# Expert blocks of two independent 128-row units, the second unit's weights copied into a ring for each pass

## The chip, the cores and the metric

The kernel runs on one core of one Trainium2 chip. The metric is the device time of one execution in microseconds (us), as the median of repeated runs. The trace is one execution taken by the hardware profiler; its engines are PE (matrix multiply; PEld is its weight load), DVE (vector), ACT (scalar activations), POOL (GpSimd) and SP, whose work here is to issue DMAs.

## The reference, cut to what matters

An input of 32 x 16 x 32 tokens of 128 channels (16,384 tokens) goes through a masked agent attention, a linear attention, and a mixture of eight experts, each with a residual. The change touches the experts alone. Of each token the router takes the two best of eight experts, and the reference adds both experts' outputs with softmax weights:

```python
logits = x @ router_w + router_b
top_w, sel = jax.lax.top_k(logits, TOP_K)            # TOP_K = 2
tok_w = zeros((T, E)).at[arange(T)[:, None], sel].add(softmax(top_w))
def body(acc, params):                               # for each of the E = 8 experts
    gu = x @ Wgu + bgu                               # 128 -> 2 x 256
    gate, up = jnp.split(gu, 2, axis=-1)
    act = (up + 1.0) * quick_gelu(gate)
    out = act @ Wd + bd                              # 256 -> 128
    return (acc + out * w_e[:, None], None)
```

## The kernel before

The kernel has three stages, one after the other, with a barrier of all engines between them: `agent_attention`, `token_mixer`, `experts`. Eight experts give 28 pairs. In `token_mixer` each token's row (128 channels and five words: two norm factors, two shares, its own number) is scattered by POOL (L810) into a DRAM tensor `rows`, in which every pair has a region of its own. Behind the last token of each region 256 rows of "nobody" are written (`tails`, L714 to L721, 14 regions from SP's queue and 14 from ACT's), so that the last block of a region is full. DVE then works out a small table (L1206 to L1238): `first_i`, where each block's rows start, and `word_i`, in which the experts of five blocks are packed as digits.

`experts` runs over 92 blocks of 256 rows, all of one pair. A block takes two passes, one for each expert of its pair, so there are 184 passes, k = 0 to 183. The engines are driven by `in_turns`: position p of the schedule holds on PE the transposes of a block's rows (`xT`, lag 1, every second position), the inner matmuls of pass p-2 (`inner`, L1366 to L1368) and the outer matmuls of pass p-4 (`outer`, L1378 to L1384). Eight positions are a turn; two turns are one iteration of the hardware loop. At the start of a turn PE reads the turn's word of experts (`look_up`, L1339). Weights are kept as a high and a low fp16 part, so a product is three matmuls. An inner pass is 12 matmuls of 256 columns, an outer pass 14 of 128 columns: for each of the two 128-row halves one for the bias and six for the hidden part. The weights' address in SBUF comes from a register, so one stationary tile serves a whole block.

DVE's `result` (L1465, lag 5) weighs a pass's output and adds it to the row. After the second pass of a block POOL scatters the block's two halves to the output (`send`, L1315 and L1318), which counts a semaphore `r_out` of the block's slot. There are eight slots. SP's `load` (L1293 to L1296) looks up a block's first row, waits for the slot's `r_out` of eight blocks earlier, and issues one DMA of 256 rows into the slot; ACT normalises them (L1400) and PE transposes them (L1351). SP's queue holds nothing else in this stage.

Of the kernel before, what the change touches and what calls it, by code (L numbers as in the profile page):

```python
# [15 lines left out]
ALU = mybir.AluOpType  # L16
# [18 lines left out]
BLOCK = 256  # L35
REGION = B * TOK + BLOCK
BLOCKS = 92
TURN = 8
TURNS = 2 * BLOCKS // TURN
SLOTS = 8  # L40
BEHIND = 4
WORDS = TURNS + 1
RSTD, SHIFT, WLO, WHI, WHO = C, C + 1, C + 2, C + 3, C + 4
ROW = C + 5
LN_STEPS, ROUTE_STEPS, EXP_STEP, PLACE_STEPS, COLUMN_STEP = 7, 14, 9, 10, 26
# [5 lines left out]
assert BLOCKS >= (B * TOK - G) // BLOCK + G and 2 * BLOCKS % TURN == 0 and TURNS % 2 == 1  # L51
# [6 lines left out]
def _constants():  # L58
# [23 lines left out]
    put(1, "next_pair", np.tile(packed[1:] - packed[:-1], (P, 5)))  # L82
    looked = (TURN * r[:, None] - BEHIND) // 2 + np.arange(5)[None, :]
    put(1, "block_no", np.concatenate([looked, r[:, None]], 1) * 1.0)
    put(1, "block_row", r[:, None] * float(BLOCK))
# [558 lines left out]

def token_mixer(nc, cst, resid, ones16, ident, mixer, ffn, rows_dram, gate_up, gate_up_bias, down, down_bias):
# [4 lines left out]
    w1_hl, w2_hl, b2_hl = ffn["w1_hl"], ffn["w2_hl"], ffn["b2_hl"]  # L650
    wall, wrow, st1 = mixer["wall"], mixer["wrow"], mixer["st1"]
    with ExitStack() as ctx:
# [41 lines left out]
        over = sb("m_over", [P, 6, G])  # L694
        found = sb("m_found", [P, 6, G])
        look = sb("m_look", [P, 6])
        cnt, cnti, nb, delta = sb("m_cnt", [P, G]), sb("m_cnti", [P, G], I32), sb("m_nb", [P, G]), sb("m_delta", [P, G])
        cum = sb("m_cum", [P, 2, G])
        word_i = sb("m_word_i", [1, WORDS], I32)
# [14 lines left out]
        b2_row = b2_hl[:].rearrange("p e c -> p (e c)")  # L714

        def tails(eng, first):

            eng.wait_ge(s.table, 2)
            for g in range(first, G, 2):
                row = eng.value_load(ffn["tail_i"][0:1, g:g + 1], min_val=g * REGION, max_val=(g + 1) * REGION - BLOCK)  # L720
                eng.dma_start(rows_dram[bass.ds(row, BLOCK)].rearrange("(n p) w -> p n w", p=P), ffn["nobody"][:]).then_inc(s.nobody_in, 16)  # L721
# [4 lines left out]
        def _(sp):  # L726
# [16 lines left out]
            sp.dma_start(rows_dram[G * REGION:G * REGION + BLOCK].rearrange("(n p) w -> p n w", p=P), ffn["nobody"][:]).then_inc(s.nobody_in, 16)  # L743
# [4 lines left out]
        def _(pool):  # L748
            g = nc.gpsimd
            g.memset(half[:], -0.5).then_inc(s.set_g, 1)  # L750
            g.memset(b2_hl[:], 0.0).then_inc(s.b_zero, 1)
# [26 lines left out]
            def biases_low(k, ring):  # L778

                if not isinstance(k, int) or k != 2:  # L780
                    return
                pool.wait_ge(s.bh_done, 1)
                g.tensor_tensor(b2_f[:], b2_f[:], b2_row[0:1, :], ALU.subtract).then_inc(s.bl_done, 1)
# [35 lines left out]
        def _(act):  # L819
# [14 lines left out]
            def biases(k, ring):  # L834
# [6 lines left out]
                if k == 1:  # L841
                    act.wait_ge(s.bf_done, 1)
                    act.wait_ge(s.b_zero, 1)
                    a.activation(b2_row[0:1, :], b2_f[:], ACT.Copy).then_inc(s.bh_done, 1)
                if k == 3:
                    act.wait_ge(s.bl_done, 1)
                    a.activation(b2_row[32:33, :], b2_f[:], ACT.Copy).then_inc(s.bh_done, 1)
# [77 lines left out]
        def _(pe):  # L925
# [108 lines left out]
            for n, column in enumerate((0, 1, 5)):  # L1034
                last = t.transpose(banks_o[0:1, 0, n * P:(n + 1) * P], look[:, column:column + 1], ident)
# [3 lines left out]
        def _(dve):  # L1039
# [30 lines left out]
            v.memset(ffn["nobody"][:].bitcast(I32)[:, :, WHO:WHO + 1], int(NO_SLOT)).then_inc(s.nobody_set, 1)  # L1070
# [137 lines left out]
            step(v.tensor_scalar(cnti[:], cnt[:], float(BLOCK - 1), None, ALU.add))  # L1208
            step(v.tensor_scalar(cnti[:], cnti[:], BLOCK.bit_length() - 1, None, ALU.arith_shift_right))
            step(v.tensor_copy(nb[:], cnti[:]))  # L1210
            step(v.tensor_scalar(delta[:], nb[:], -float(BLOCK), float(REGION), ALU.mult, ALU.add), False)
# [6 lines left out]
            all_pairs = [P, 6, G]  # L1218
            number = const(cst, "block_no").rearrange("p (n o) -> p n o", o=1).to_broadcast(all_pairs)
            step(v.tensor_tensor(over[:], number, now.rearrange("p (o g) -> p o g", o=1).to_broadcast(all_pairs), ALU.is_ge))  # L1220
            step(v.tensor_tensor(found[:, 0:5, :], over[:, 0:5, :], const(cst, "next_pair").rearrange("p (n g) -> p n g", n=5), ALU.mult), False)
            step(v.tensor_tensor(found[:, 5, :], over[:, 5, :], delta[:], ALU.mult))
            step(v.tensor_reduce(look[:], found[:], AX.X, ALU.add))

            step(v.tensor_scalar(look[:, 0:5], look[:, 0:5], 1.0, None, ALU.add), False)
            step(v.tensor_tensor(look[:, 5:6], look[:, 5:6], const(cst, "block_row"), ALU.add))
            step(v.tensor_scalar(look[:, 5:6], look[:, 5:6], float(G * REGION), None, ALU.min), False)
            step(v.scalar_tensor_tensor(look[:, 0:1], look[:, 1:2], 64.0, look[:, 0:1], ALU.mult, ALU.add))
            step(v.scalar_tensor_tensor(look[:, 0:1], look[:, 2:3], 4096.0, look[:, 0:1], ALU.mult, ALU.add), False)
            step(v.scalar_tensor_tensor(look[:, 1:2], look[:, 4:5], 64.0, look[:, 3:4], ALU.mult, ALU.add))  # L1230
            dve.wait_ge(s.col_psum, 1)
            row = banks_o[0:1, 0]
            word = ffn["word_i"]
            step(v.tensor_copy(ffn["first_i"][:], row[:, 2 * P:2 * P + BLOCKS]), False)
            step(v.tensor_copy(word[:], row[:, 0:WORDS]), False)
            step(v.tensor_copy(word_i[:], row[:, P:P + WORDS]))
# [5 lines left out]
def in_turns(eng, *stages, look=None):  # L1242
# [11 lines left out]
    with eng.Fori(0, TURNS // 2) as two:  # L1254
# [267 lines left out]
```

## Time and profile before

| | |
|---|---|
| median of 3 runs | 1207.85 us (1205.22 to 1208.79) |
| profiled execution | 1216.59 us, its span 1214.8 us |
| `agent_attention`, `token_mixer`, `experts`, us from the span's start | 0 to 371, 371 to 763, 763 to 1214.8 |
| PE busy over the span | 1034.6 us, 85% |
| DVE busy | 891.0 us, 73% |
| ACT busy | 714.4 us, 59% |
| POOL busy | 583.1 us, 48% |
| DMA | 64.18 MB, mean 53 GB/s |

The span is 1.8 us less than the profiled execution, which is 8.7 us above the median. A busy share is an average over three stages of different kinds; what the last stage is bound by is read in the last stage.

### The profile page before, as it was taken

What the parts mean: (1) busy time and instruction counts of PE and PEld (TensorE: products, weight loads), DVE (VectorE), ACT (ScalarE), POOL (GpSimd) and SP (SyncE); (2) the same over time, 40 slices, a digit from 0 to 9 for tenths busy, and PEclk for the clock granted to TensorE, in tenths of its full rate; (3) what the DMA queues carried; (4) which work ended last, traced back from release to release, by engine and by line L of the source; (5) the groups of instructions that cost most, each with busy time, mean ns of one, the idle gap of its engine ahead of it and who ended that gap; (6) DMA issues with size and microseconds to landing.
All of it is one profiled execution on the core that took longest, in us unless ns stands there. A gap on an engine that the chain in (4) does not pass through costs nothing. (4 is left out here: it accounts for less than half of the span.)

```text
span 1214.8 us, 39840 instructions
## 1 busy us (share of the span) xinstructions
PE 1034.6 (85%) x12967; PEld 857.2 (71%) x12968; DVE 891.0 (73%) x2181; ACT 714.4 (59%) x1446; POOL 583.1 (48%) x630
## 2 busy tenths in 40 slices
PE   5799999999986887888887840699999999999995
PEld 4477877787763456666666740588888898888984
DVE  5687777777773347877877762488888888888985
ACT  1277665666643257676676620567676767676763
POOL 0425746374676215555655552144444444444443
PEclk9899999999997778999999965799999999999998
DMA  8011101011103001111211219221112111221110
GB/s 308 26 38 28 38 21 35 21 37 29 29 3 105 18 18 41 59 58 59 68 51 60 65 56 142 55 57 50 52 55 56 51 52 48 56 56 52 35 23 1
DMA packets 72324, 64.18 MB, mean 53 GB/s; under 512 B 9812, under 2 KB 58227, under 8 KB 72237
## 3 DMA queue, kind: packets, MB, share of 16 engines
q1 hardware_dynamic: 57132, 43.46, 13.3%
q0 software_dynamic: 10016, 17.16, 4.6%
q10 hardware_dynamic: 5090, 2.32, 1.5%
q8 instruction: 64, 1.05, 0.4%
q14 instruction: 22, 0.18, 0.1%
HBM read 33.44 MB, written 24.72 MB: 48 GB/s over the span
## 5 line engine op out<-in xcount | busy, mean ns | idle before, releaser
L1318 POOL DMA_INDIRECT out<-e_y,e_xg x184 | 183.7, 998 | 77.8 <-issue 77.6
L1366 PE MATMUL e_ps<-e_xt,w_hl 128*128 128x256 f16 x736 | 202.2, 275 | 14.2 <-issue 12.8
L1367 PE MATMUL e_ps<-e_xt,w_hl 128*128 128x256 f16 x736 | 201.8, 274 | 0.0
L1368 PE MATMUL e_ps<-e_xt,w_hl 128*128 128x256 f16 x736 | 201.7, 274 | 0.0
L810 POOL DMA_INDIRECT rows<-m_rows,m_place x128 | 127.5, 996 | 44.4 <-issue 44.4
L251 POOL TENSOR_SCALAR vm<-v,early 128x512 f32<-128x512 f32 x96 | 148.5, 1562 | 0.0
L1383 PE MATMUL e_ps<-w_hl,e_hid_hl 128*128 x736 | 145.6, 220 | 0.0
L1384 PE MATMUL e_ps<-w_hl,e_hid_hl 128*128 x736 | 144.9, 219 | 0.0
L1382 PE MATMUL e_ps<-w_hl,e_hid_hl 128*128 x736 | 144.1, 220 | 0.0
L1443 DVE SCALAR_TENSOR_TENSOR e_hid_hl<-e_hid,e_hid_hl 128x512 f16<-128x512 f32 x184 | 127.4, 692 | 20.0 <-ACT e_hid_hl L1416 19.7
L1437 DVE SCALAR_TENSOR_TENSOR e_hid<-e_ps,e_act 128x512 f32<-128x512 f32 x184 | 125.9, 684 | 15.2 <-ACT e_act L1422 10.9
L1416 ACT ACTIVATE e_hid_hl<-e_hid 128x512 f16<-128x512 f32 x184 | 115.2, 626 | 16.6 <-DVE e_hid L1437 7.0
L1422 ACT ACTIVATE e_act<-e_ps 128x512 f32<-128x512 f32 x184 | 107.8, 586 | 9.9 <-PE e_ps L1368 9.8
L1400 ACT ACTIVATE e_xn<-e_xg 128x128 f32<-128x128 f32 x184 | 80.2, 489 | 42.1 <-DMA e_xg<-rows 42.1
L249 POOL TENSOR_TENSOR vm<-v,early 128x512 f32<-128x512 f32 x32 | 33.2, 1039 | 135.5 <-PE ps L447 132.3
L1315 POOL TENSOR_TENSOR e_held<-e_one 1x1 f32<-1x1 f32 x92 | 18.3, 199 | 162.9 <-DVE e_y L1465 162.9
L1409 ACT ACTIVATE e_xt<-e_ps 128x256 f16<-128x256 f32 x92 | 35.2, 383 | 102.5 <-PE e_ps L1351 102.5
L1366 PEld LDWEIGHTS e_ps<-e_xt,w_hl 128*128 x736 | 72.2, 98 | 28.6 <-issue 18.4
L286 ACT ACTIVATE km<-ps,bk_pair,early 128x512 f32<-128x512 f32 x128 | 89.1, 789 | 0.0
L1378 PE MATMUL e_ps<-b_hl,e_ones 128*128 x368 | 80.6, 219 | 0.7 <-DVE e_hid_hl L1443 0.7
L1368 PEld LDWEIGHTS e_ps<-e_xt,w_hl 128*128 x736 | 72.4, 98 | 8.8
L1367 PEld LDWEIGHTS e_ps<-e_xt,w_hl 128*128 x736 | 72.4, 98 | 6.8
(249 smaller groups left out, 2603.6 us busy)
## 6 DMA issues: line engine op xcount, KB each, us to landing
e_xg<-rows SPq DMA_DIRECT2D x92, 133.0 KB
resid<-in_x SPq DMA_DIRECT2D x8, 1024.0 KB, 13.9
xb<-in_x SPq DMA_DIRECT2D x32, 256.0 KB, 2.7
m_rows<-resid SPq DMA_DIRECT2D x32, 256.0 KB, 2.7
out<-e_y,e_xg POOLq DMA_INDIRECT x184, 2.3
m_w_f<-in_L_ffn_gate_up_proj SPq DMA_DIRECT2D x1, 2048.0 KB, 8.2
rows<-m_rows,m_place POOLq DMA_INDIRECT x128, 2.4
rows<-nobody SPq DMA_DIRECT2D x15, 133.0 KB, 10.0
```

What stands on the lines that cost most here:

```text
L251: ins = g.tensor_scalar(vm[:, u, :, n, :], full, pair_of[:, n:n + 1], None, ALU.mult)
L810: g.indirect_dma_start(rows_dram, bass.IndirectOffsetOnAxis(ap=place[:, slot, j:j + 1], axis=0), rows[:, slot, j, :], None).then_inc(s.row ...
L1318: nc.gpsimd.indirect_dma_start(out_rows, bass.IndirectOffsetOnAxis(ap=who, axis=0), y[:, slot, i, :], None, bounds_check=B * TOK - 1, oob_ ...
L1366: t.matmul(o, hi, x2[0], start=True, stop=False)
L1367: t.matmul(o, hi, x2[1], start=False, stop=False)
L1368: last = t.matmul(o, lo, x2[0], start=False, stop=True)
L1382: t.matmul(o, hi, whi, start=False, stop=False)
L1383: t.matmul(o, hi, wlo, start=False, stop=False)
L1384: last = t.matmul(o, lo, whi, start=False, stop=q == 1)
L1416: a.activation(hid_hl[:, i, 0].rearrange("p q n -> p (q n)"), hid[:, i], ACT.Copy, scale=1.0 / (WS * QG)).then_inc(s.hh_done, 1)
L1437: v.scalar_tensor_tensor(hid[:, i], ps[:, 4 + i], WS, act_g[:, i], ALU.add, ALU.mult).then_inc(s.hid_done, 1)
L1443: v.scalar_tensor_tensor(hid_hl[:, i, 1].rearrange("p q n -> p (q n)"), hid[:, i], 1.0 / (WS * QG), hid_hl[:, i, 0].rearrange("p q n -> p ...
```

## The change

A unit is now 128 rows of one pair. A block is still 256 rows and two passes, but it is any two units, whose pairs need not agree. There are 78 blocks (156 units, 156 passes) in place of 92 blocks (184 passes). The tail of nobody rows is 128 rows for each region.

The two halves of a block may need different experts in one pass. The first half takes its weights as before, by a register. For the second half SP copies one expert's packed weights (1664 fp16 numbers on each of 128 partitions, 416 KB in all) from `weights` to one of eight places of a ring `e_fed`, once for each pass; PE waits for that copy before the pass's inner matmuls. Of a block, SP loads the two halves with a DMA each, each with its own look-up, which now stands behind the wait for `r_out`. The copies of block b stand in SP's queue behind the load of block b+4 (`LEAD = 4`), and each waits for the outer matmuls of eight passes earlier.

The inner matmuls become 24 of 128 columns for each pass (12 of 256 before); the outer ones stay 14 of 128. The table gets two starts for each block and a second word for each turn: twelve searched columns in place of six, six small transposes in place of three, three more steps on DVE.

```diff
+UNIT = 128
-BLOCK = 256
-REGION = B * TOK + BLOCK
-BLOCKS = 92
+BLOCK = 2 * UNIT
+REGION = B * TOK + UNIT
+BLOCKS = 78
+LEAD = 4
...
         def tails(eng, first):
...
-                eng.dma_start(rows_dram[bass.ds(row, BLOCK)].rearrange("(n p) w -> p n w", p=P), ffn["nobody"][:]).then_inc(s.nobody_in, 16)
+                eng.dma_start(rows_dram[bass.ds(row, UNIT)], ffn["nobody"][:]).then_inc(s.nobody_in, 16)
...
             def load(n, slot, rounds):
 
-                row = sp.value_load(ffn["first_i"][0:1, n:n + 1] if isinstance(n, int) else ffn["first_i"][0:1, bass.ds(n, 1)],
-                                    min_val=0, max_val=G * REGION)
                 need(sp, r_out[slot], 32 * rounds)
-                sp.dma_start(xg[:, slot], rows_dram[bass.ds(row, BLOCK)].rearrange("(n p) w -> p n w", p=P)).then_inc(x_in[slot], 16)
+                for half in range(2):
+                    row = sp.value_load(ffn["first_i"][0:1, half, at(n)], min_val=0, max_val=G * REGION)
+                    sp.dma_start(xg[:, slot, half], rows_dram[bass.ds(row, UNIT)]).then_inc(x_in[slot], 16)
+
+            def second_words(turn):
+
+                return sp.value_load(ffn["word_i"][0:1, 1, at(turn)], min_val=0, max_val=64 ** 5 - 1)
+
+            def second_weights(k, ring, word, digit):
+
+                e = (word // 8 ** (digit + 1 - 2 * (digit % 2))) % 8
+                need(sp, s.y_psum, k - TURN + 1)
+                sp.dma_start(fed[:, ring:ring + 1], ffn["weights"][:, bass.ds(e, 1)]).then_inc(fed_in[ring], 16)
+
+            def eight(m, first, last, loads):
+
+                word = None
+                for i in range(first, last):
+                    if i < loads:
+                        load(SLOTS * m + i, i, m)
+                    if i < LEAD and isinstance(m, int) and m == 0:
+                        continue
+                    turn = -1 if i < 3 else 0 if i < 7 else 1
+                    if word is None or i in (3, 7):
+                        word = second_words(2 * m + turn)
+                    for u in range(2):
+                        far = 2 * (i - LEAD) + u
+                        second_weights(2 * SLOTS * m + far, far % TURN, word, far - TURN * turn + BEHIND)
...
-                x2 = [xt[:, slot % 2, l, :] for l in range(2)]
+                pe.wait_ge(fed_in[j], 16 * (2 * rounds + slot // 4) + 16)
...
+                        for half in range(2):
+                            x2 = [xt[:, slot % 2, l, half * P:(half + 1) * P] for l in range(2)]
+                            o = ps[:, bank + i, q * BLOCK + half * P:q * BLOCK + (half + 1) * P]
+                            if half:
+                                hi, lo = (w1_fed[:, j, l, at:at + P] for l in range(2))
```

On SP's queue, inside the loop over blocks, this is what stood for one block before (`first_i` is the table of starts, `e_xg` the slots' rows, `e_r1_out` the count of slot 1's scatters):

```order
L1293 ISA
L1293 TENSOR_LOAD first_i
L1293 ISA x2
L1296 ISA [waits e_r1_out]
L1296 DMA e_xg<-rows 128x2x133
```

Now the same place reads as follows (`e_fed` is the ring, `e_y_psum` counts PE's outer passes; left out is the second half's look-up, which repeats the first's).

```order
L1314 ISA [waits e_r1_out]
L1314 TENSOR_LOAD first_i
L1314 ISA x2
L1315 ISA
L1315 DMA e_xg<-rows 128x133
...
L113 REGISTER_ALU
L1325 ISA [waits e_y_psum]
L1325 DMA e_fed<-weights 128x1664
L113 REGISTER_ALU
L1325 ISA [waits e_y_psum]
L1325 DMA e_fed<-weights 128x1664
```

The look-up has moved behind the wait for the slot, there are two loads, and two copies of weights stand behind them; in three blocks of eight a look-up of the word of experts (`word_i`) stands between loads and copies.

On PE this is the start of an inner pass before (`e_act_done` says that a bank of PSUM is free):

```order
L110 REGISTER_ALU [waits e_xl_done,e_xh_done]
L1366 ISA [waits e_act_done]
L1366 MATMUL e_ps<-e_xt,w_hl 128x256
L1367 MATMUL e_ps<-e_xt,w_hl 128x256
L1368 ISA
L1368 MATMUL e_ps<-e_xt,w_hl 128x256
```

and now (`weights` holds the eight experts, `e_fed4_in` counts the landings of the ring's fifth place):

```order
L113 REGISTER_ALU [waits e_fed4_in,e_xl_done,e_xh_done]
L1413 ISA [waits e_act_done]
L1413 MATMUL e_ps<-e_xt,weights 128x128
L1414 MATMUL e_ps<-e_xt,weights 128x128
L1415 ISA
L1415 MATMUL e_ps<-e_xt,weights 128x128
L1413 MATMUL e_ps<-e_xt,e_fed 128x128
L1414 MATMUL e_ps<-e_xt,e_fed 128x128
L1415 MATMUL e_ps<-e_xt,e_fed 128x128
```

Each matmul has become two of half the width, and the wait for the copy stands ahead of the pass's first matmul, with all later work of PE behind it.

## Rows read from the trace of the kernel before

**Rows 1.** Stretches: us, busy us by engine (instructions), PE clock granted, DMA share, GB/s.
```profile
0.00:30.00 30.00, 15.72 (x93) 11.93 (x94) 15.90 (x41) 3.48 (x5) 1.32 (x6) 1.00 0.86 312
488.00:709.00 221.00, 180.36 (x1252) 145.99 (x1250) 175.10 (x654) 144.64 (x347) 125.69 (x159) 0.98 0.19 59
780.00:1200.00 420.00, 407.15 (x4861) 371.47 (x4859) 370.18 (x810) 294.68 (x626) 197.22 (x270) 1.00 0.18 48
```

**Rows 2.** Timeline of PE, one pass (start us, us); the page's inner weight loads (ns).
```profile
906.19 0.27 PE L1366 MATMUL e_ps<-e_xt,w_hl 128*128 128x256 f16 x1
...
907.50 0.22 PE L1378 MATMUL e_ps<-b_hl,e_ones 128*128 x1
...
908.28 0.39 PE L1351 MATMUL e_ps<-early,e_xn 128*128 128x128 f32 x2
908.51 0.27 PE L1366 MATMUL e_ps<-e_xt,w_hl 128*128 128x256 f16 x1
...
L1366 PEld LDWEIGHTS e_ps<-e_xt,w_hl 128*128 x736 | 72.2, 98 | 28.6 <-issue 18.4
```

**Rows 3.** Timelines of PE: the first inner matmul of block 0 and of block 91.
```profile
769.29 0.39 PE L1366 MATMUL e_ps<-e_xt,w_hl 128*128 128x256 f16 x1 [1.33 <-DVE e_xt L1451]
...
1194.96 0.28 PE L1366 MATMUL e_ps<-e_xt,w_hl 128*128 128x256 f16 x1 [0.41 <-issue]
```

**Rows 4.** Timelines of PE, DVE, POOL, SP: block 27's end, the load that waits for it.
```profile
901.78 0.27 PE L1366 MATMUL e_ps<-e_xt,w_hl 128*128 128x256 f16 x1
...
906.58 0.34 DVE L1465 SCALAR_TENSOR_TENSOR e_y<-e_ps,e_xg,e_y 128x128 f32<-128x128 f32 x1
...
907.99 1.00 POOL L1318 DMA_INDIRECT out<-e_y,e_xg  x1 [0.54 <-issue]
909.29 0.98 POOL L1318 DMA_INDIRECT out<-e_y,e_xg  x1 [0.30 <-issue]
...
911.72 0.37 SPq L1296 DMA_DIRECT2D e_xg<-rows  x1
...
915.50 0.28 PE L1366 MATMUL e_ps<-e_xt,w_hl 128*128 128x256 f16 x1 [0.33 <-issue]
```

**Rows 5.** Lines of SP: ns min/median/max, first and last start us; then two starts.
```profile
L1293 SPq TENSOR_LOAD <-first_i x92: 263/268/281, 763.3 to 1168.4; - x92
L1296 SPq DMA_DIRECT2D e_xg<-rows x92: 371/373/1047, 764.1 to 1172.6; - x92
...
764.07 0.41 SPq L1296 DMA_DIRECT2D e_xg<-rows  x1
772.73 0.37 SPq L1296 DMA_DIRECT2D e_xg<-rows  x1
```

**Rows 6.** DMA landings: of `e_xg` (min/median/max us); on the page, count, KB, median us.
```profile
DMA to landing us min/median/max: 2.1/2.3/3.7
...
xb<-in_x SPq DMA_DIRECT2D x32, 256.0 KB, 2.7
m_rows<-resid SPq DMA_DIRECT2D x32, 256.0 KB, 2.7
```

**Rows 7.** Nobody rows: SP's lines, landings, SP's wait; the DMA of 728 to 766.
```profile
L720 SPq TENSOR_LOAD <-tail_i x14: 278/372/565, 729.0 to 745.9; - x14
L721 SPq DMA_DIRECT2D rows<-nobody x14: 372/372/413, 729.9 to 746.6; - x14
DMA to landing us min/median/max: 3.1/10.3/16.3
SPq L652 <- DMA rows<-nobody: 15.9, 1, 15.9
DMA packets 8210, 4.65 MB, mean 122 GB/s; under 512 B 624, under 2 KB 8048, under 8 KB 8208
rows<-m_rows,m_place POOLq DMA_INDIRECT x9, 9.6
```

**Rows 8.** Timeline of POOL: its last scatter of rows in `token_mixer`.
```profile
741.14 0.96 POOL L810 DMA_INDIRECT rows<-m_rows,m_place  x1 [0.30 <-issue]
```

## What the change will do, predicted before any run of it

> **What bounds the kernel now.** I read the stretches first, then PE's timeline in the last stage, then the one other thing that the change leans on there, SP's queue. From 780 to 1200 us PE is busy 407 of 420 us at the full granted clock, DVE 370, ACT 295, and the DMA engines 18% of the time at 48 GB/s [rows 1]. So the last stage is PE's, with DVE close behind and much room in the DMA engines. One pass on PE: the twelve inner matmuls run from 906.19 to 907.50, 1.31 us or 109 ns each; the fourteen outer ones from 907.50 to 908.28, 0.78 us or 56 ns each; a block's two transposes take 0.23 us [rows 2]. Two passes and the transposes are 4.41 us. Block 0 starts its inner matmuls at 769.29 and block 91 at 1194.96 [rows 3]: 425.7 us over 91 intervals, 4.68 us a block. The 0.27 us over 4.41 is lost where a turn begins and PE reads its word.
>
> The second thing to see is how late a slot comes free. In one steady block, 27, DVE begins the last result at 906.58, 4.80 us after PE started the next block's inner matmuls at 901.78; POOL issues the two scatters at 907.99 and 909.29, and SP's load that waits for them starts at 911.72, 5.14 us after the result [rows 4]. That wait costs nothing today: the rows loaded there are used almost four blocks later. PE starts block 31, four later, at 915.50, 8.9 us after that result [rows 4].
>
> **The change, part by part.** Fewer blocks. If PE stayed the bound, 77 intervals would take the place of 91. A pass has 24 inner matmuls of 128 columns at the 56 ns of the outer ones, 1.34 us in place of 1.31; a block grows by 0.06 to 4.74, and 77 of them are 365 us, 61 us less than now.
>
> A rule speaks against that pitch. The Trainium skill, TensorE: Matmul & The Clock Gate, section Back-to-back issue gap, says that a stream of weight load and matmul pairs of 128 columns sustains about 81 ns each. The fourteen pairs of an outer pass run at 56 ns here, so the trace does not agree, and by the rule it is a rival below.
>
> The copies and their place in SP's queue. This is the step on which I expect the gain to be lost. Copies of block b stand behind the load of block b+4, which waits for the scatters of block b-4. So PE may not start block b until a chain has run from the last result of block b-4. Its links:
> - to the point where SP's first load of the block would start: 5.14 us [rows 4].
> - SP's own work. In the start of the stage, where loads wait for nothing, eight loads start between 764.07 and 772.73; seven intervals are 8.66 us, and one of the DMAs took 1.05 in place of 0.37, so an undisturbed load with its look-up is (8.66 - 0.67) / 7 = 1.14 us [rows 5]. The look-up is some 0.62 of it (1.14 less the DMA's 0.37 and about 0.15 of register steps and gaps), and it moves behind the wait. Then comes the second half's load, which I take at 1.10 (half the pieces), 0.6 until the first copy starts, and in three blocks of eight a look-up of the word, 0.62 x 3/8 = 0.23. Together 2.55.
> - the copy's landing. A load of 133 KB lands after 2.3 us, copies of 256 KB from DRAM or within SBUF after 2.7 [rows 6]. At 312 GB/s with the engines 86% busy [rows 1] the DMA moves 363 GB/s, so 416 KB (426,000 bytes) take 1.17 us, 0.45 more than 256 KB: 3.15 by that, 2.3 as the lower end. No row shows a 416 KB copy; I take 2.9, nearer to the copy within SBUF, whose rows are in four times as many pieces.
> - 0.2 us until PE's first matmul, and 0.2 because copies and scatters now share the engines (estimates; the second is one 0.2 us piece of a scatter's data).
>
> The sum is L = 5.14 + 2.55 + 2.9 + 0.4 = 11.0 us. The last result of block b-4 begins A = 4.8 us after the start of block b-3 [rows 4], 4.9 with the longer inner passes and PE's restart behind a wait. So block b starts at least A + L = 15.9 us after block b-3: three blocks take 15.9, one takes 5.30. PE alone needs 4.74, which would allow L up to 3 x 4.74 - 4.9 = 9.3. PE therefore waits about 0.55 us in each block, and 77 x 5.30 = 408.1 replace 425.7: **-17.6 us** in place of -61. Queued behind the waiting matmul are all of PE's later work and through it DVE, ACT and POOL; as the chain runs through them, it does not catch up.
> The second copy of a block starts 0.6 us after the first and is needed a pass (2.2 us) later, so it hides. The DMA engines carry two copies (2.35 us) and today's 18% in 5.3 us, some 60%: not the bound.
>
> The start of the stage. SP's first look-up starts at 763.3, its first load at 764.07 [rows 5], PE's first inner matmul at 769.29 [rows 3], 6.0 later. Now the first copy stands behind five blocks' loads: 0.73 + nine intervals of 1.10 + 0.37 for the last DMA, then the word 0.65 and 0.2 to the copy, 11.85; with 2.9 to land and 0.2 for PE 14.95. **+9.0 us**. Nothing hides it, as no other work is there yet. Later copies of the first four blocks come at 1.7 us a pass or less and keep ahead of PE.
>
> The nobody rows. SP's last of fourteen DMAs starts at 746.6, but SP waits 15.9 us for their landings, up to 762.9 [rows 7]. In 728 to 766 us 4.65 MB moved, of which 28 x 0.136 = 3.8 MB are nobody rows; the queue is late because of bytes. Half of them leave 2.75 MB. If the data took 30.5 us (from about 730 to 2 us before the wait ends), they take 18 now and end near 748, 2 us later landed: 750. SP's own issue ends at 746.6 less 14 x 0.04, plus 3.1 for the shortest landing, 749; POOL's last scatter starts at 741.14 and lands in 9.6 at today's load [rows 7, 8], 750.7, and no later with less load. The barrier opens about 750.5 in place of 763: **-12.5 us**, between -14 and -9.
>
> The table. Three more steps, wider searches and three more transposes are 1 to 2 us on DVE and PE that end near 740, under the nobody rows that end at 750; uncovered they would cost 2 us. The strided weights cost nothing that I can name, and the end of the kernel is as before.
>
> **Sum.** -17.6 + 9.0 - 12.5 = -21.1 us. The profiled execution of 1216.6 becomes 1195.5; it stands 8.7 above the median, so the median becomes **1187 us**.
>
> **Bounds.** Lower: landing 2.3, no sharing, 0.1 for PE: L 10.1, A 4.8, 4.97 a block, 383 us; with the rest -46, or 1162. Upper: landing 3.7 (the longest of a load), look-ups at the 0.565 us seen under a loaded queue in place of 0.27 [rows 7], 2.4 of them, and scatters 0.5 later: L 12.8, A 5.0, 5.93 a block, 457 us, +31 + 9 - 9 = +31, or 1239.
>
> **Rivals.**
> The copies are hidden. Then 365 us, -61 + 9 - 12.5 = -64, 1143 us. It needs L under 9.3; 5.14 and SP's 2.55 alone are 7.7, and no DMA in the rows lands in 1.4.
> Slower, by the same chain. The whole gain is gone when a block takes 425.7 + 3.5 over 77, 5.57 us, which is from L = 11.8 on. Loaded look-ups and landings of 3.4 us are enough: L 12.4, 5.77 a block, 444 us, +18.6 + 9 - 12.5 = +15, 1223 us. For it speaks that look-ups doubled under load; against it that the engines are 40% free.
> Weight loads that show. A load takes 98 ns [rows 2] and hides behind 109 ns of an inner matmul now. If in a stream of 24 pairs it did not hide, inner passes would be 24 x 98 = 2.35 us and a block 6.5, over the chain's 5.3: 500 us, +75 + 9 - 12.5 = +71, 1279 us. The outer passes hide the same loads behind 56 ns. By the page's 81 ns a block would be 6.4 us, much the same.
> PE's clock falls. Waiting 0.55 us in each block, PE is busy some 85%; between 488 and 709 us it was busy 82% at a mean granted clock of 0.98 [rows 1]. If a tenth of the stage ran at 1.2 GHz, where a block's 4.5 us of matmuls doubles, that tenth would take 8 x 9.3 us for 8 x 5.3: +32, 1219 us.
> That the change does less work than it says can't be: the number of blocks is fixed in the loops.
>
> **Chances.** Chain as summed 0.66 (1164 to 1208 us), hidden 0.06, slower by the chain 0.17, weight loads 0.05, clock 0.06. The range leaves out the hidden case, the weight loads and the far end of the slow ones: 1164 to 1219. About 0.3%, 3.6 us, is what a measurement of this kernel can tell from no change. Inside 1204.2 to 1211.5 lies a part of the chain's case and of the slower one, 0.09; faster 0.69, slower 0.22.
>
> **What would show it.** Right: PE's inner matmuls of a block's first pass wait about 0.55 us for a DMA of `e_fed`, every block alike from block 4 on; blocks 5.3 us apart; a result 15.9 - 4.9 = 11 us ahead of the inner matmul four blocks later; the barrier at 750; the first inner matmul 15 us behind it. Wrong: no waits of PE on `e_fed` and blocks 4.74 apart (the chain is shorter than its rows); matmuls 80 ns apart; waits on every pass, and the DMA share near one (bytes); a clock under one.

## The result, and the profile after

The changed kernel takes 1222.7 us (median of 4 runs, 1217.1 to 1223.9) where the kernel before took 1207.1 beside it (4 runs, 1205.2 to 1208.8): a ratio of 1.0121, 95% interval 1.0085 to 1.0156. A second set of runs on another chip gave 1.0105, 1.0082 to 1.0128. The change is slower by about 1.1%, outside the predicted range and on the other side of zero. The profiled execution took 1222.6 us with a span of 1220.7; before, the span was 1214.8.

The last stage, by stretch. The columns are those of [rows 1].

```profile
780.00:1200.00 420.00, 352.07 (x5664) 334.79 (x5662) 306.06 (x654) 244.93 (x510) 158.69 (x217) 0.97 0.53 193
```

PE was busy 407 of these 420 us before [rows 1], and is busy 352 now; no other engine is near its limit, and the DMA engines are 53% busy. So nothing is full, and something is late. What is late is in the list of waits of the same stretch (engine, line, what ended the wait: us in total, times, longest).

```profile
POOL e_held L1357 <- DVE e_y L1516: 200.9, 73, 6.0
ACT e_xt L1460 <- PE e_ps L1393: 93.8, 70, 2.7
PEld e_ps L1413 <- issue: 77.9, 59, 3.2
ACT e_act L1473 <- PE e_ps L1415: 64.8, 49, 3.9
POOL out L1360 <- issue: 61.3, 144, 2.0
PE e_ps L1413 <- DMA e_fed<-weights: 55.8, 37, 3.1
```

The last line is the one to read: PE waits for a copy of the weights 37 times, 1.5 us each, in the 73 blocks of the stretch. POOL (through DVE), ACT and the weight loads wait for PE in turn.

PE's first inner matmul of block 0, and then that of block 77, from PE's timeline (start us, us; in brackets the idle time before it):

```profile
761.62 0.29 PE L1413 MATMUL e_ps<-e_xt,weights 128*128 128x128 f16 x1 [9.96 <-DMA e_fed<-weights]
...
1203.35 0.22 PE L1413 MATMUL e_ps<-e_xt,weights 128*128 128x128 f16 x1
```

That is 441.7 us over 77 intervals, 5.74 us a block, against 425.7 us before [rows 3]. The prediction had 408.1 and 5.30.

One turn of the chain, from the timelines of PE, DVE, POOL, SP and PE again. Block 33 starts, block 32 gives its last result, its two scatters go, SP loads block 40, copies for block 36, and PE starts block 36:

```profile
953.62 0.23 PE L1413 MATMUL e_ps<-e_xt,weights 128*128 128x128 f16 x1 [1.56 <-DMA e_fed<-weights]
...
958.46 0.60 DVE L1516 SCALAR_TENSOR_TENSOR e_y<-e_ps,e_xg,e_y 128x128 f32<-128x128 f32 x2
...
959.88 1.00 POOL L1360 DMA_INDIRECT out<-e_y,e_xg  x1 [0.55 <-issue]
961.19 0.98 POOL L1360 DMA_INDIRECT out<-e_y,e_xg  x1 [0.30 <-issue]
...
965.07 1.55 SPq L1315 DMA_DIRECT2D e_xg<-rows  x2
967.62 1.31 SPq L1325 DMA_DIRECT2D e_fed<-weights  x2
...
970.85 0.23 PE L1413 MATMUL e_ps<-e_xt,weights 128*128 128x128 f16 x1 [0.19 <-issue]
```

From block 33's start to block 36's it is 17.23 us for three blocks, 5.74 each, which is the mean pace. Its parts are A = 958.46 - 953.62 = 4.84 and L = 970.85 - 958.46 = 12.39. The prediction named this ring and every link of it; it had L = 11.0. In the profile's records the copy for block 36 has landed at 970.53, and PE's matmuls of the blocks before end at 970.66 and leave 0.19 us of idle time: in this turn the copy and PE's own work come out almost together. Of the 61 blocks from 8 to 69 whose landing can be told, PE starts 42 within 0.6 us of the copy's landing, 0.41 us behind it on average; the others it starts later for reasons of its own, as where it reads its word.

Two more places answer to the rest of the sum. The nobody rows: SP's line, the landings, and SP's wait at the barrier, as in [rows 7].

```profile
L731 SPq DMA_DIRECT2D rows<-nobody x14: 332/332/381, 727.2 to 742.1; - x14
DMA to landing us min/median/max: 2.0/3.7/4.2
...
SPq L662 <- DMA rows<-nobody: 3.5, 1, 3.5
```

The wait fell from 15.9 us to 3.5 and the median landing from 10.3 to 3.7. And SP's look-ups of rows (ns min/median/max, first and last start) with the copies' DMAs and their landings:

```profile
L1314 SPq TENSOR_LOAD <-first_i x156: 264/290/894, 746.3 to 1179.7; - x156
...
L1325 SPq DMA_DIRECT2D e_fed<-weights x156: 485/496/1316, 758.5 to 1193.5; - x156
DMA to landing us min/median/max: 2.7/2.7/3.7
```

The first look-up is at 746.3, 17.0 us before the 763.3 of [rows 5]; PE's first inner matmul comes 15.3 us after it, where it was 6.0.

### The profile page after: what moved, and what is told of

Same layout as the page of the kernel before. It is cut to its first block and busy times, and to the rows that moved or that the text cites. A ratio compares the mean times of both kernels' runs of the same rounds, so it can differ in the third digit from the quotient of the medians.

```text
span 1220.7 us, 41928 instructions
## 1 busy us (share of the span) xinstructions
PE 995.1 (82%) x14086; PEld 837.9 (69%) x14087; DVE 841.5 (69%) x2058; ACT 673.9 (55%) x1348; POOL 552.6 (45%) x588
## 5 line engine op out<-in xcount | busy, mean ns | idle before, releaser
L1413 PE MATMUL e_ps<-e_xt,weights 128*128 128x128 f16 x624 | 139.6, 224 | 79.1 <-DMA e_fed<-weights 65.8
L1360 POOL DMA_INDIRECT out<-e_y,e_xg x156 | 155.7, 998 | 65.7 <-issue 65.7
L1488 DVE SCALAR_TENSOR_TENSOR e_hid<-e_ps,e_act 128x512 f32<-128x512 f32 x156 | 107.2, 687 | 86.7 <-PE e_ps L1415 66.4
L1415 PE MATMUL e_ps<-e_xt,weights 128*128 128x128 f16 x624 | 139.6, 224 | 0.0
L1415 PE MATMUL e_ps<-e_xt,e_fed 128*128 128x128 f16 x624 | 139.1, 223 | 0.0
L1414 PE MATMUL e_ps<-e_xt,e_fed 128*128 128x128 f16 x624 | 139.1, 223 | 0.0
L1413 PE MATMUL e_ps<-e_xt,e_fed 128*128 128x128 f16 x624 | 139.0, 223 | 0.0
L1414 PE MATMUL e_ps<-e_xt,weights 128*128 128x128 f16 x624 | 138.9, 223 | 0.0
L1413 PEld LDWEIGHTS e_ps<-e_xt,weights 128*128 x624 | 62.0, 99 | 93.0 <-issue 89.6
L1494 DVE SCALAR_TENSOR_TENSOR e_hid_hl<-e_hid,e_hid_hl 128x512 f16<-128x512 f32 x156 | 108.1, 693 | 16.7 <-ACT e_hid_hl L1467 15.8
L1467 ACT ACTIVATE e_hid_hl<-e_hid 128x512 f16<-128x512 f32 x156 | 97.7, 626 | 14.1 <-DVE e_hid L1488 7.1
L965 PE MATMUL m_ps<-wall,m_xt 128*128 128x256 f32 x256 | 67.6, 411 | 5.4 <-DVE m_kf L1132 5.3
L965 PEld LDWEIGHTS m_ps<-wall,m_xt 128*128 128x128 f32 x256 | 49.7, 204 | 24.2 <-issue 17.9
L1434 PE MATMUL e_ps<-weights,e_hid_hl 128*128 x312 | 64.6, 225 | 0.0
```

The lines of the kernel that those rows point to most:

```text
L965: last = t.matmul(banks_kv[:, j // 2, j % 2 * 2 * C:(j % 2 + 1) * 2 * C], xt[:, u, j * P:(j + 1) * P], wall[:, C:3 * C], start=True, stop= ...
L1360: nc.gpsimd.indirect_dma_start(out_rows, bass.IndirectOffsetOnAxis(ap=who, axis=0), y[:, slot, i, :], None, bounds_check=B * TOK - 1, oob_ ...
L1413: t.matmul(o, hi, x2[0], start=True, stop=False)
L1414: t.matmul(o, hi, x2[1], start=False, stop=False)
L1415: last = t.matmul(o, lo, x2[0], start=False, stop=True)
L1467: a.activation(hid_hl[:, i, 0].rearrange("p q n -> p (q n)"), hid[:, i], ACT.Copy, scale=1.0 / (WS * QG)).then_inc(s.hh_done, 1)
```

## The experiments

Each kernel was run beside the kernel before on the same chip. That kernel's median was 1207 us on the first chip and 1213 to 1216 on the others, so I compare kernels by us a block (first inner matmul of block 0 to that of block 77, over 77), which moves little from chip to chip: the changed kernel unaltered, on another chip, has 5.745.

> The changed kernel unaltered, on the chip of the run beside it: ratio to the kernel before 1.012 and 5.74 us a block if the first result holds from chip to chip.

Measured: 1225.95 us, ratio 1.0105 (1.0082 to 1.0128), 5.745 a block. The result holds.

**The place in SP's queue.** My theory was that the pace is the ring's length over the number of blocks in it. The first edit puts one block more into the ring:

```
                 for i in range(first, last):
-                    if i < loads:
-                        load(SLOTS * m + i, i, m)
                     if i < LEAD and isinstance(m, int) and m == 0:
+                        load(SLOTS * m + i, i, m)
                         continue
...
                         second_weights(...)
+                    if i < loads:
+                        load(SLOTS * m + i, i, m)
```

> The two copies of block b stand ahead of the load of block b+4 in SyncE's queue instead of behind it, so that they wait on the scatters of block b-5 and no longer on those of b-4. Theory (the ring of result, scatter, load, copy, inner matmul sets the pace: (4.9 + 12.4) / 3 = 5.77 us a block, measured 5.74): with one block more in the ring it would be 17.3 / 4 = 4.3, below what TensorE needs by itself, about 4.75; so 77 x (5.74 - 4.75) = 76 us go and the time is about 1147, with next to no wait of TensorE for a copy. Rival one (the 32 KB a partition that the copies move for each ring turn slow everything, whatever order): the same bytes in the same time, so above 1200. Rival two (the narrower matmuls of 128 columns set the pace): the same, about 1222.

Measured: 1160.5 us, ratio 0.953 (0.949 to 0.957), 4.92 us a block. The same copies of the same size, in another place of the queue, give back 63 us of the stage (77 x 0.82). Waits of PE on the copies, 780 to 1110 us:

```profile
PE e_ps L1414 <- DMA e_fed<-weights: 6.3, 6, 1.2
```

It is not the 4.75 that I expected; the last experiments take that up. The opposite edit is `LEAD = 5`, with the second turn of eight blocks written out:

```
-LEAD = 4
+LEAD = 5
...
             eight(0, 0, SLOTS, SLOTS)
-            with sp.Fori(1, BLOCKS // SLOTS) as m:
+            eight(1, 0, SLOTS, SLOTS)
+            with sp.Fori(2, BLOCKS // SLOTS) as m:
```

> The copies of block b stand behind the load of block b+5, which waits for the scatters of b-3: one block less in the ring (the second turn of eight blocks is written out, so that its waits are constants). Theory: 17.4 us of ring over two blocks in place of three, less up to 0.5 us a ring for copies and scatters that now meet less often: 8.4 to 8.7 us a block, 77 x (8.4 to 8.7 - 5.74) = 205 to 228 us more, 1428 to 1450. If the order in the queue were not the cause, the same as the changed kernel, or less, for fewer copies in the same time.

Measured: 1449.9 us in one run, 8.61 a block. From 780 to 1420 us PE's waits and the stretch (columns of [rows 1]):

```profile
PE e_ps L1414 <- DMA e_fed<-weights: 244.1, 35, 8.7
...
780.00:1420.00 640.00, 395.86 (x5645) 388.39 (x5642) 301.14 (x652) 241.65 (x508) 159.19 (x218) 0.79 0.35 127
```

Every second block waits some 7 us. Over blocks 8 to 69 the mean A is 5.79 and L 12.2, so the ring gives 18.0 / 2 = 9.0, and the measured mean there is 9.04. A is longer than in the changed kernel because PE comes back from such a wait at half clock: the mean granted clock is 0.79 here, and the matmuls of the block at 900.97 us stand 107 ns apart until 902.36. With two blocks in the ring 8.6, with three 5.74, with four 4.92 (where the ring alone would allow 4.3 and so no longer binds): the place in the queue sets the pace.

**The length of the ring.** Two edits shorten it and leave the order alone. The first looks both row numbers up ahead of the wait:

```
+                found = [sp.value_load(ffn["first_i"][0:1, half, at(n)], ...) for half in range(2)]
                 need(sp, r_out[slot], 32 * rounds)
                 for half in range(2):
-                    row = sp.value_load(ffn["first_i"][0:1, half, at(n)], ...)
-                    sp.dma_start(xg[:, slot, half], rows_dram[bass.ds(row, UNIT)]).then_inc(x_in[slot], 16)
+                    sp.dma_start(xg[:, slot, half], rows_dram[bass.ds(found[half], UNIT)]).then_inc(x_in[slot], 16)
```

> SyncE looks both row numbers up before it waits for the scatters, as the kernel before did; the copies stay behind the load. Theory: from the wake to the first load's issue 0.87 us falls to about 0.3, and from the first issue to the second 1.21 falls to about 0.5, so the ring loses about 1.2 us: (4.9 + 11.2) / 3 = 5.37 a block, 77 x 0.37 = 29 us less, about 1194. Rival one (bytes of the copies): no change, 1215 to 1225. Rival two (narrow matmuls): no change.

Measured: 1199.8 us, ratio 0.987 (0.985 to 0.989), 5.39 a block. L is 11.30 (mean over blocks 8 to 69), 1.07 less; a third of that is 0.36 and the pace fell by 0.35. Two look-ups moved ahead of a wait are worth 27 us of the stage, and turn the change from 1% slower into 1.3% faster than before.

The second leaves the order and the wait and takes the bytes away (in this kernel and the next two both units take the first unit's weights, lines that the cuts leave out):

```
-                sp.dma_start(fed[:, ring:ring + 1], ffn["weights"][:, bass.ds(e, 1)])...
+                sp.dma_start(fed[:, ring:ring + 1, 0:WB], ffn["weights"][:, bass.ds(e, 1), 0:WB])...
```

> Each copy moves only the 256 bytes a partition of the bias instead of 3,328, in the same place of SyncE's queue, and TensorE waits for it as before; both units take the first unit's weights, which is the part left out. It tells what the size of the copies costs from what their place in the queue costs. Theory: the ring stays, and loses only what the traffic adds to it, about 0.65 us on the scatters' landing and about 0.6 on the copy's own: (4.9 + 11.1) / 3 = 5.35 us a block, about 1192. If the traffic were the main cost, the pace would fall to TensorE's own, 4.7, and the time to about 1145; if it cost nothing, 5.74 and 1222.

Measured: 1180.8 us in one run, 5.18 a block, better than the 5.35 expected. The links of the ring, means over blocks 8 to 69 from the timelines, beside what the prediction had:

| link, us | predicted | changed kernel | small copies |
|---|---|---|---|
| last result to first load's DMA | 5.14 + 0.62 = 5.76 | 6.74 | 6.11 |
| first load to second | 1.10 | 1.23 | 1.21 |
| second load to first copy | 0.60 + 0.23 = 0.83 | 0.89 | 0.89 |
| copy's issue to PE's first matmul | 2.9 + 0.2 = 3.1 | 3.50 | 2.48 |
| allowed for sharing | 0.2 | in the links | in the links |
| L | 11.0 | 12.37 | 10.69 |
| A | 4.9 | 5.04 | 4.89 |
| (A + L) / 3 | 5.30 | 5.80 | 5.19 |

So the size of the copies is worth 1.68 us of L: 1.0 in the copy itself, 0.64 between result and load, 0.03 between the loads. The rest of the ring is order, and stays with copies of 32 KB. SP's look-ups of rows (780 to 1200 us) in the changed kernel, then with the small copies, and the small copies' landings:

```profile
L1314 SPq TENSOR_LOAD <-first_i x138: 264/301/894, 781.5 to 1179.7; - x138
...
L1314 SPq TENSOR_LOAD <-first_i x139: 263/277/422, 780.8 to 1139.1; - x139
DMA to landing us min/median/max: 1.7/1.8/3.4
```

**The traffic without the wait, and the matmuls alone.** In the next kernel PE takes the wait for the copy in `outer`, two passes later:

```
             def inner(k, n, j, slot, rounds):
-                pe.wait_ge(fed_in[j], 16 * (2 * rounds + slot // 4) + 16)
...
             def outer(k, n, j, slot, rounds):
                 need(pe, s.hl_done, k + 1)
+                pe.wait_ge(fed_in[j], 16 * (2 * rounds + slot // 4) + 16)
```

> Every copy is issued in the changed kernel's place and waited for, but by TensorE only ahead of the second product of the pass, some 5 us later than there, and both units take the first unit's weights. So the whole traffic stays and the ring gets slack. Theory: ring (4.9 + 12.4 - 5) / 3 = 4.1, under TensorE's own pace, so 4.9 us a block as where the copies stand ahead of the load, and first inner matmul sooner by 8 us: about 1150. If the traffic itself set the pace: above 5.3 a block, above 1185.

Measured: 1156.4 us in one run, 4.96 a block, with the full traffic (225 GB/s from 780 to 1110 us). The last kernel of this group drops the copies too:

```
-                need(sp, s.y_psum, k - TURN + 1)
-                sp.dma_start(fed[:, ring:ring + 1], ffn["weights"][:, bass.ds(e, 1)]).then_inc(fed_in[ring], 16)
+                return
```

> Leaves out the copies and the wait for them, and both units of a block take the first unit's weights (so the second unit's rows meet another pair's weights); the loads and the narrow matmuls stay. Theory: TensorE's own pace shows, about 4.75 us a block, and the start waits for no copy (first inner matmul about 7 us after SyncE's first look-up instead of 15.3): 1222 - 76 - 8 = about 1138. Rival two (narrow matmuls set the pace): 5.7 a block stays, about 1214.

Measured: 1137.8 us in one run, 4.71 a block, first inner matmul 6.7 us after the first look-up. From 780 to 1110 us PE is as busy as the kernel before is in that stretch (319.78 us):

```profile
780.00:1110.00 330.00, 320.90 (x5469) 312.73 (x5467) 289.20 (x633) 231.35 (x492) 153.66 (x210) 1.00 0.20 53
```

The matmuls of 128 columns cost what the prediction said (4.74). Of the 1.03 us a block between 4.71 and 5.74, 0.77 go when only the wait moves, and 0.26 stay with the copies, that is with their bytes or with SP's work of issuing them. They do not slow the matmuls as such: over blocks 8 to 69 four blocks of eight take 4.47 to 4.49 us with these copies as without any, and what is left lies in the blocks in which PE reads its word and the ones right behind.

**A version that beats both.** Copies of block b behind the load of block b+1 or b+2 wait for scatters of blocks long done, and go out early in the stage:

```
-LEAD = 4
+LEAD = 1
...
-                    turn = -1 if i < 3 else 0 if i < 7 else 1
-                    if word is None or i in (3, 7):
+                    turn = -1 if i < LEAD - 1 else 0 if i < LEAD + 3 else 1
+                    if word is None or i in (LEAD - 1, LEAD + 3):
```

> The copies of block b stand behind the load of block b+1, not b+4: they wait only for the ring slot of b-4 (its second product), and in the steady state for no scatter younger than block b-7's. The first copies go out after two loads instead of five. Theory: TensorE's own pace and its dearer look-ups, 4.8 to 4.9 us a block (as with the copies ahead of the load, 4.90), and a first inner matmul some 6 us sooner, 9 us behind SyncE's first look-up: 1160 - 6 - 4 = about 1150, a ratio of 0.946 to the kernel before. If something other than the place in the queue holds the copies, 1160 or more.

Measured: 1147.6 us (1146.0 to 1150.6), ratio 0.9454 to the kernel before, interval 0.9433 to 0.9475; 4.81 a block, first inner matmul 8.3 us behind the first look-up, and no wait of PE on a copy from 780 to 1120 us. One constant, with the look-up places that follow from it, turns a loss of 1.1% into a gain of 5.5%.

> The same with the copies of block b behind the load of b+2, which waits for the scatters of b-6. Theory: the pace of the kernel above within 0.1 us a block, the first inner matmul 2 us later than there: about 1152. It tells whether the slack that the order gives is used up at one block (as where the copies stand just ahead of the load of b+4) or more.

Measured: 1146.2 us in one run, 4.84 a block, first inner matmul 10.5 us behind the first look-up: the same kernel in time.

**What holds the pace then.** Where the copies stood ahead of the load, 4.92 was left instead of 4.71. Two things stood out there. SP no longer waits: from 780 to 1110 us its list of waits is one line, where the changed kernel has 68.5 us on the scatters. And PE's look-ups of its word are slow. SP's waits of the changed kernel, then of the kernel with the copies ahead of the load; PE's look-ups (780 to 1200 us, ns min/median/max) without copies, and with the copies ahead of the load:

```profile
SPq L1314 <- DMA out<-e_y,e_xg: 68.5, 40, 3.7
...
SPq L1325 <- PE e_ps L1436: 0.2, 1, 0.2
...
L1380 PEldq TENSOR_LOAD <-word_i x18: 297/300/367, 788.4 to 1108.4; - x18
...
L1382 PEldq TENSOR_LOAD <-word_i x18: 302/754/946, 796.9 to 1131.1; - x18
```

To take work from SP I packed a block's two row numbers into one word (the last two lines are shortened):

```
+            both = ffn["first_i"]
+            step(v.tensor_copy(both[:], firsts[:, 0:2, 0:BLOCKS]))
+            step(v.tensor_scalar(both[:, 0], both[:, 0], 7, None, ALU.logical_shift_right))
+            step(v.tensor_scalar(both[:, 1], both[:, 1], 5, None, ALU.logical_shift_left))
+            step(v.tensor_tensor(both[:, 0], both[:, 0], both[:, 1], ALU.bitwise_or))
...
+                two = sp.value_load(ffn["first_i"][0:1, 0, at(n)], ...)
+                for half, row in enumerate((two % 4096 * UNIT, two // 4096 * UNIT)):
```

> The same packing with the copies just ahead of the load of block b+4, where a block took 4.90 to 4.92 us. Two causes of the 0.2 over TensorE's own 4.70 are open: SyncE's own instructions, or TensorE's look-ups of the word, 0.72 us each in place of 0.31 while copies move (0.1 a block). If SyncE: 4.70 to 4.80 a block, about 1150. If only the look-ups: 4.90 and 1160 as before.

Measured, with the copies ahead of the load of b+4: 1151.1 us (1147.6 to 1155.3), ratio 0.947 (0.944 to 0.950), 4.82 a block, as the theory on SP had it. The pace is from one trace of each kernel, and the two intervals of the ratio touch. But PE's look-ups became fast in the same run (0.34 us on average, 0.72 without the packing), probably because copies that go out earlier no longer meet them. The look-ups' 0.38 us in every fourth block are 0.1 a block, as much as was gained. What was taken out of the stage is SP's second look-up alone, so SP's own instructions stand behind the gain; how much of the 0.1 was PE's look-up and how much a late copy stays open.

> As the run with the copies behind the load of block b+2, and the two row numbers of a block packed into one word (three more small VectorE steps in the table), so that SyncE looks up once a block. In that run, and where the copies stood ahead of the load, SyncE was without a wait almost throughout: its own instructions, about 4.8 us a block, kept pace with TensorE's. Theory: SyncE falls to about 4.1 us a block and TensorE alone sets the pace, 4.70 to 4.78 (4.835 before), with idle time again in SyncE's queue; start 0.6 us sooner: about 1141, ratio to the kernel before 0.940. If SyncE was not a bound: 4.83 and 1146 or more.

Measured: 1148.7 us (1146.4 to 1149.9, 5 runs), ratio 0.9462 (0.9439 to 0.9484), 4.80 a block. This expectation was wrong. SP has idle time again,

```profile
SPq L1329 <- PE e_ps L1439: 40.3, 48, 1.6
SPq L1317 <- DMA out<-e_y,e_xg: 13.8, 22, 2.1
```

but PE runs at the pace it had without the packing. With the copies behind the load of b+2 SP was full and yet in nobody's way. Against the 4.71 without copies 0.09 a block are left. Over blocks 8 to 69 that is 0.70 us in eight blocks, of which 0.43 lie in the two blocks in which PE reads its word (the longer takes 5.62 us in place of 5.35) and 0.17 in the ones right behind, and no run tells what they are.

## Why the prediction was wrong

By its own steps, on the profiled executions (the change measured +5.9 us in span, 1214.8 to 1220.7):

- **What bounds it now, and what will:** right. The ring was named with its links, its divisor of three, the place of the wait and its effect on the engines behind PE. The runs with two, three and four blocks in the ring show that it is the cause.
- **The pace of the blocks: the step that failed.** Its sum gave -17.6 us and the stage gave 441.7 - 425.7 = +16.0, an error of 33.6. The failed term is L, 11.0 against 12.37; a third of the 1.4 us, on each of 77 blocks, is 36 us, with A's 0.14 some 39 (the mean over blocks 8 to 69; over all 77 intervals 33.6). Most of the 1.4 is the link from the last result to the first load, 6.74 us for 5.76. The two links behind it have 0.19 more, the copy's 0.40, and the 0.2 that I had allowed for sharing comes off.
  - My rows were too short for this queue even without traffic. With small copies the first three links still have 8.20 against my 7.69, 0.35 of it between result and load. That is not for a badly chosen block: over blocks 4 to 79 of the kernel before this link has a mean of 5.15, block 27 of [rows 4] 5.14. The look-up behind the wait starts 2.61 us after the second scatter, where the load itself started 2.39 after it before, and from the look-up's start to the load it is 0.74 where I had 0.62.
  - Traffic cost more than I allowed. With it the first three links grow by another 0.67, where I had allowed 0.2: the first look-up behind the wait takes 0.52 us on average in place of 0.28, and starts 3.00 us after the second scatter in place of 2.61.
  - The copy's link has 0.40 more than my 2.9 + 0.2, but not by its landing, which took 2.79 us on average: PE's first matmul comes 0.69 us behind the landing where I had 0.2, 0.41 in the 42 blocks in which PE is ready for it and longer in the rest.
- **The reason for which I set the slower case low** was that the engines are 40% free. That is a mean. A copy occupies them all while it runs. The share of the DMA engines from 907 to 913 us, in 40 slices of 0.15 us (9 is 90% or more):

```profile
DMA  5999998600000000047940000499404999999899
```

They are full for 1 us, idle for more than another, busy for half of one, and then, behind a copy's issue at 910.43, full for most of the time from 910.9 to 913. Of the 62 first look-ups behind the wait (blocks 8 to 69), 41 took over 0.4 us. While these ran, the engines were nearly all busy (0.99 on average); while the other 21 ran, 0.39. The rival with L = 12.4 and 5.77 a block, 1223 us, is nearest to what happened, but of the two causes it named only the loaded look-ups are seen; landings of 3.4 us are not. That its 12.4 meets the 12.37 is in part luck, and so is its 1223: the misses below on the nobody rows, the end and the median are in its sum too, and they nearly cancel.
- **The start of the stage:** right, 15.3 us for 14.95.
- **The nobody rows:** right in kind, and the size is nearer than it looks. The first look-up is 17.0 us sooner for my 12.5, but 2.7 of this lie ahead of the rows: SP's first DMA of the fourteen starts at 727.2 where it was 729.9. From there to the first look-up it was 33.4 us and is 19.1, so 14.3 less, 0.3 outside the bounds of -14 and -9. And this trace is the shortest of all: the same kernel on another chip has 21.6 there, and the other kernels of the experiments have 21.0 to 22.7, that is 10.7 to 12.4 less than before.
- **The end:** 17.4 us from the last block's start to the end of the span in place of 19.8, which I had put at no change: -2.4.
- **From the profiled execution to the median:** I took 8.7 us off because the profiled execution before stood so far above its median. The one after stands on its median, so 8.9 us of the miss come from this step, which had no mechanism behind it. The sum of the misses is 33.6 - 4.5 + 0.4 - 2.4 + 8.9 = 36.0, and the miss is 1222.7 less the 1186.8 that I had rounded to 1187, 35.9.
- **The clock:** a small part of that rival came true. The mean is 0.97, and behind six of the longest waits PE runs for some us at 1.2 GHz. Behind a wait of 2.3 us its matmuls are 107 ns apart in place of 56, and that block has an A of 6.4 us. Six blocks of the 62 have an A of 6.1 to 6.5; each began behind a wait for a copy of 2.1 to 3.1 us, and the mean granted clock over its first 3 us is 0.50 to 0.72. The one at 867 us (0.50 from its start to 870.17; the stretch shown begins in the wait):

```profile
867.17 0.28 PE L1413 MATMUL e_ps<-e_xt,weights 128*128 128x128 f16 x1 [2.32 <-DMA e_fed<-weights]
867.25 0.31 PE L1414 MATMUL e_ps<-e_xt,weights 128*128 128x128 f16 x1
867.36 0.31 PE L1415 MATMUL e_ps<-e_xt,weights 128*128 128x128 f16 x1
...
866.50:869.50 3.00, 2.33 (x23) 2.33 (x24) 0.02 (x1) 0.60 (x1) 1.95 (x2) 0.61 0.58 198
```

- **Weight loads that show:** excluded, as the trace had it: the 24 inner matmuls that start at 953.62 stand 56.5 ns apart, the last at 954.92, and a block takes 4.71 without copies. The twenty-second to the twenty-fourth of them:

```profile
954.81 0.22 PE L1413 MATMUL e_ps<-e_xt,e_fed 128*128 128x128 f16 x1
954.87 0.22 PE L1414 MATMUL e_ps<-e_xt,e_fed 128*128 128x128 f16 x1
954.92 0.22 PE L1415 MATMUL e_ps<-e_xt,e_fed 128*128 128x128 f16 x1
```

The rule of the Trainium skill, TensorE: Matmul & The Clock Gate, section Back-to-back issue gap, of about 81 ns a pair, is not borne out here.
- **"Every block alike":** not so. The waits are 0 to 3 us and blocks 4.5 to 7.1 apart, in a pattern of about eight blocks. A look-up of the word, or a turn of PE's loop, falls on some of them, which fits it.

The range failed with the forecast. L's upper bound of 12.8 was worked out and held the truth, yet the range ended at 1219, as I gave the slower case 0.17 and cut it off. The decision was between L = 11.0 and 11.8, and a ring of six links, each known to 0.1 or 0.2 us and nearly all with an error to the same side, does not support 0.69 on one side of it.

## What to carry to other kernels

When a transfer is put into an in-order queue behind a wait, work out the ring that this closes, and the number of items in it: here the number (two, three, four blocks) was worth far more than any link, and moving the copies three loads forward was worth 6%. Where an error in a link is multiplied by the number of blocks, take its duration from rows that are loaded as the new kernel will load them, not from the start of a stage where nothing else runs. Look-ups that depend on nothing belong ahead of the wait.

## What the runs showed of the hardware

A look-up of a word from SBUF into a register slows down while large copies within SBUF run. With the copies ahead of the load, PE's took 0.75 us at the median and up to 0.95 in place of 0.30; SP's, within 3 us behind the issue of a copy, 0.55 at the median in place of 0.27. With copies of 32 KB both stay at 0.28 to 0.31 at the median and on average, so it is the bytes in flight and not the number of DMAs. (The Trainium skill, DMA: Bandwidth & Descriptors, section Latency and other measured facts, gives `tensor_load` a floor of about 600 ns; the rows here go down to 264 ns, and the measurement decides.) A copy of 416 KB within SBUF landed in 2.7 us at the median in the changed kernel (up to 3.7, and up to 5.0 with the copies ahead of the load) and one of 32 KB in 1.8 (up to 3.4), so of a small one most does not hang on its bytes. And SP's queue can be full with DMAs of two units and two copies a block: in the run with `LEAD = 1` the gaps of over 0.15 us between its instructions sum to 2.2 of the 300 us from 800 to 1100 (65 in the changed kernel), at 4.8 us a block. What SP does there is two look-ups and two load DMAs of 0.34 us, two copy DMAs of 0.50, and the register steps between them.
